# A five-layer graph transformer on one core: edge one-hots built once and loaded from DRAM in each layer

## What is computed

```python
k = typed_linear(x, ntype, Wk).reshape(n, H, HD)
q = typed_linear(x, ntype, Wq).reshape(n, H, HD)
v = typed_linear(x, ntype, Wv).reshape(n, H, HD)
kw = typed_linear_heads(k[src], etype, att)
a = jnp.sum(kw * q[dst], axis=-1) * pri[:, etype].T / np.float32(np.sqrt(HD))
amax = jax.ops.segment_max(a, dst, num_segments=n)
ae = jnp.exp(a - amax[dst])
w = ae / jax.ops.segment_sum(ae, dst, num_segments=n)[dst]
m = typed_linear_heads(v[src], etype, msg) * w[:, :, None]
h = jax.ops.segment_sum(m, dst, num_segments=n).reshape(n, D)
h = typed_linear(h, ntype, Wa)
return h * alpha + x * (1 - alpha)
```

## Time and profile before

| | us |
|---|---|
| median of 3 runs | 9909.2 |
| lowest and highest run | 9865.0, 9917.3 |
| span of the profiled execution | 9921.5 |
| PE busy | 5554.4 (56%) |
| DVE busy | 4643.5 (47%) |
| POOL busy | 4557.4 (46%) |
| ACT busy | 4066.5 (41%) |
| the five edge loops, each | 1512 to 1571 |

### The profile page before, as it was taken

One profiled execution on the slowest core, in us unless ns is written; L12 is line 12 of the kernel. 1 busy time (PEld: TensorE's weight loads), 2 busy tenths in 40 slices (PEclk: granted clock), 3 DMA queues, 4 the chain that ended last, 5 costly groups with the idle time before them and its releaser, 6 DMA issues.

```text
span 9921.5 us, 147395 instructions
## 1 busy us (share of the span) xinstructions
PE 5554.4 (56%) x33354; PEld 4735.9 (48%) x33355; DVE 4643.5 (47%) x12764; ACT 4066.5 (41%) x10084; POOL 4557.4 (46%) x4797
## 2 busy tenths in 40 slices
PE   5654545586554555955555559445454594555554
PEld 3544444464444444744444447344444573444443
DVE  5254545532555555235554552355555523555555
ACT  1244444432444444324444443344444433444442
POOL 0345555433455554335555542445555424555553
PEclk9866676797677666977666679767767796676667
DMA  2322222213222221232222213222222132222221
GB/s 69 144 62 70 70 71 70 68 70 125 69 71 72 71 72 56 100 107 72 69 72 72 69 45 124 93 69 71 70 70 71 37 140 83 73 74 73 73 76 36
DMA packets 272656, 761.00 MB, mean 77 GB/s; under 512 B 87871, under 2 KB 104356, under 8 KB 271908
## 3 DMA queue, kind: packets, MB, share of 16 engines
q0 software_dynamic: 199680, 545.53, 19.2%
q1 hardware_dynamic: 72228, 208.51, 5.4%
HBM read 557.87 MB, written 195.88 MB: 76 GB/s over the span
## 4 chain that ended last, share of the span: by engine, by line
PE 31%; another core or an unknown queue 25%; DVEq 16%; issue 12%; DVE 10%; POOLq 3%; ACT 2%; ACTq 1%; DMA 0%; POOL 0%; SPq 0%
PE ps L535 6%; PE ps L627 6%; DVEq L1061 5%; DVEq L1051 5%; PE ps L643 4%; PE ps L648 4%; PE ps L552 3%; POOLq L459 3%; DVEq L228 2%; PE ps L555 2%; PE ps L588 1%; PE ps L642 1%; DVE prod L1045 1%; DVE wmsg L1025 1%
## 5 line engine op out<-in xcount | busy, mean ns | idle before, releaser
L443 POOL DMA_INDIRECT rows<-table,idx_now x4160 | 3981.4, 957 | 3529.5 <-DVE wmsg L1029 1878.9
L642 PE MATMUL ps<-zeros,identb 128*128 128x132 bf16 x2080 | 555.0, 267 | 3189.9 <-DVE wmsg L1029 2780.9
L704 ACT ACTIVATE prod<-iota_n,dloc 128x128 bf16<-128x128 f32 x6240 | 1988.9, 389 | 106.0 <-issue 78.7
L642 PEld LDWEIGHTS ps<-zeros,identb 128*128 128x128 bf16 x2080 | 242.1, 116 | 3353.3 <-issue 3171.5
L1045 DVE TENSOR_TENSOR prod<-ps,rows 128x512 f32<-128x512 f32 x1040 | 715.5, 688 | 2352.6 <-remote 1820.4
L709 ACT ACTIVATE ohf<-prod,ones 128x512 f32<-128x512 bf16 x1040 | 750.5, 722 | 2326.4 <-remote 1887.0
L627 PE MATMUL ps<-qn,ohT 128*128 x8320 | 1583.6, 350 | 67.8 <-issue 62.7
L627 PEld LDWEIGHTS ps<-qn,ohT 128*128 128x128 f32 x8320 | 1407.3, 255 | 135.9 <-issue 129.7
L643 PE MATMUL ps<-wmsg,ohf 128*128 128x132 f32 x4160 | 1267.6, 398 | 0.0
L648 PE MATMUL ps<-wmsg,ohf 128*128 128x132 f32 x4160 | 1090.9, 355 | 0.0
L588 PE MATMUL ps<-identb,oh 128*128 128x128 bf16 x4160 | 531.8, 268 | 730.4 <-ACT ohT L721 358.8
(11 more groups left out here) (162 smaller groups left out, 6391.4 us busy)
## 6 DMA issues: line engine op xcount, KB each, us to landing
table<-rows SPq DMA_DIRECT2D x245, 768.0 KB, 3.2
rows<-table,idx_now POOLq DMA_INDIRECT x4160
out<-h SPq DMA_DIRECT2D x1, 3072.0 KB
wk<-in_L_gnn_Wk SPq DMA_DIRECT2D x20, 48.0 KB
wq<-in_L_gnn_Wq SPq DMA_DIRECT2D x20, 48.0 KB
wv<-in_L_gnn_Wv SPq DMA_DIRECT2D x20, 48.0 KB
wa<-in_L_gnn_Wa SPq DMA_DIRECT2D x20, 48.0 KB
attw<-in_L_gnn_rel_att SPq DMA_DIRECT2D x20, 24.0 KB
```

The lines of the kernel that those rows point to most:

```text
L443: pool.indirect_dma_start(out=rows[:, slot, j, :], out_offset=None, in_=table, in_offset=bass.IndirectOffsetOnAxis(ap=idx_now[:, half, c:c ...
L642: pe.matmul(bank[:, AW:2 * AW], identb[:], zeros[:], start=True, stop=True)
L704: act.activation(squares[:, turn % 2, j * P:(j + 1) * P], iota_n[:], ACT.Square, bias=dloc[:, at(4 * q + j)], scale=-1.0)
```

## The change

Everything about the one-hots leaves the edge loop. After the preparation a new stage of 208 groups, `batches`, with four buffers in the memory of `rows`, makes them once: DVE compares iota with `dloc` for four chunks in one instruction (`gen_oh`), SP stores this to `oh_d` in DRAM, PE turns it, ACT copies the turned form in bf16 (`gen_ohT`), SP stores it to `ohT_d`. In the edge loop SP loads, per position, one 128 x 512 bf16 piece of `ohT_d` for this step and one of `oh_d` for the sum two positions on, each into one of two buffers (`ohTb`, `ohb`); ACT casts each to fp32, into the same `ohT` and `ohf` as before. `dloc` moves from a buffer of its own into the memory of `rows`. SP's issues of the next layer's weights now stand ahead of the one-hot loads, and its waits for them behind the loop.

```diff
+GB = 4
+    oh_d = nc.dram_tensor("oh_d", (QUADS, P, 4 * P), BF16, kind="Internal").ap()
+    ohT_d = nc.dram_tensor("ohT_d", (QUADS, P, 4 * P), BF16, kind="Internal").ap()
...
-        oh = sb("oh", [P, 2, 4, P], BF16)
+        ohb = sb("ohb", [P, 2, 4 * P], BF16)
+        ohTb = sb("ohTb", [P, 2, 4 * P], BF16)
...
+        def batches(eng, body):
+            for k in range(GB):
+                body(k, k, 0)
+            with eng.Fori(0, QUADS // GB - 1) as it:
+                for k in range(GB):
+                    body(it * GB + (GB + k), k, it + 1)
...
             def edges_(l):
                 wa_load(l)
+                if not isinstance(l, int):
+                    weights(l + 1)
+                def body(q, slot, use, n):
+                    b = slot % 2
+                    if not beyond(q):
+                        if not is_first(q, 2):
+                            hold(sp, s_ohT, l * QUADS + q - 1)
+                        sp.dma_start(ohTb[:, b, :], ohT_d[at(q), :, :].rearrange("q p c -> (q p) c")
+                                     ).then_inc(s_ohTl[b], 16)
+                    a = summed(q + 2)
+                    if a is not None:
+                        if not is_first(a, 2):
+                            hold(sp, s_ohf, l * QUADS + a - 1)
+                        sp.dma_start(ohb[:, b, :], oh_d[at(a), :, :].rearrange("q p c -> (q p) c")
+                                     ).then_inc(s_ohl[b], 16)
+                positions(sp, body)
                 hold(sp, s_wa, l * (16 * R4) + 16 * R4)
...
+            def keep(q, b, use):
+                hold(sp, s_goh, q + 1)
+                sp.dma_start(oh_d[at(q), :, :].rearrange("q p c -> (q p) c"), gen_oh[:, b, :]).then_inc(s_gst[b], 16)
+                hold(sp, s_gohT, q + 1)
+                sp.dma_start(ohT_d[at(q), :, :].rearrange("q p c -> (q p) c"), gen_ohT[:, b, :]).then_inc(s_gst[b], 16)
+            batches(sp, keep)
+            for b in range(GB):
+                sp.wait_ge(s_gst[b], 32 * (QUADS // GB))
...
+            def turn_onehots(q, b, use):
+                pe.wait_ge(s_goh, q + 1)
+                if not is_first(q, GB):
+                    pe.wait_ge(s_gohT, q - (GB - 1))
+                for j in range(4):
+                    last = pe.transpose(ps[:, b, :].bitcast(BF16)[:, j * P:(j + 1) * P],
+                                        gen_oh[:, b, j * P:(j + 1) * P], identb[:])
+                last.then_inc(s_gtr, 1)
+            batches(pe, turn_onehots)
...
                     if not beyond(q):
-                        act.wait_ge(s_ohp, l * QUADS + q + 1)
+                        act.wait_ge(s_ohTl[b], l * (QUADS // 2 * 16) + (use * (RING // 2) + slot // 2) * 16 + 16)
                         if not is_first(q, 2):
                             act.wait_ge(s_qe, l * QUADS + q - 1)
-                        act.copy(ohT[:, b].rearrange("p s c -> p (s c)"),
-                                 ps[:, 0, :].bitcast(BF16)[:, 0:4 * P]).then_inc(s_ohT, 1)
+                        act.copy(ohT[:, b].rearrange("p s c -> p (s c)"), ohTb[:, b, :]).then_inc(s_ohT, 1)
...
                     if a is not None:
-                        onehot(ohf, a, 1 - b, turn + 1 + b, None if is_first(a, 2) else l * QUADS + a - 1).then_inc(s_ohf, 1)
+                        loads = use * (RING // 2) + (slot + 1) // 2 - LAG // 2
+                        act.wait_ge(s_ohl[1 - b], l * (QUADS // 2 * 16) + loads * 16 + 16)
+                        if not is_first(a, 2):
+                            act.wait_ge(s_agg, l * QUADS + a - 1)
+                        act.copy(ohf[:, 1 - b].rearrange("p s c -> p (s c)"), ohb[:, 1 - b, :]).then_inc(s_ohf, 1)
...
+            def make_onehots(q, b, use):
+                if not is_first(q, GB):
+                    dve.wait_ge(s_gst[b], use * 32)
+                dve.tensor_tensor(
+                    gen_oh[:, b, :].rearrange("p (s c) -> p s c", s=4),
+                    iota_n[:].rearrange("p (s c) -> p s c", s=1).broadcast_to((P, 4, P)),
+                    dloc[:, at(4 * q, 4)].rearrange("p (s c) -> p s c", c=1).broadcast_to((P, 4, P)),
+                    ALU.is_equal).then_inc(s_goh, 1)
+            batches(dve, make_onehots)
...
-                    if b == 1 and not beyond(q + 2):
-                        dve.wait_ge(s_ohp, l * QUADS + q + 1)
-                        onehot(q + 2, b).then_inc(s_oh[b], 1)
```

More of the change, by code:

```diff
@@ L182, in gnn @@
         s_gath = [sem(f"gathered{i}") for i in range(RING)]
-        s_oh = [sem(f"onehot_ready{i}") for i in range(2)]
-        s_ohp = sem("onehot_transposed")
-        s_ohT = sem("onehot_copied")
+        s_ohl = [sem(f"onehot_loaded{i}") for i in range(2)]
+        s_ohTl = [sem(f"onehot_t_loaded{i}") for i in range(2)]
+        s_ohT = sem("onehot_t_widened")
+        s_goh = sem("onehot_made")
+        s_gtr = sem("onehot_turned")
+        s_gohT = sem("onehot_t_made")
+        s_gst = [sem(f"onehot_stored{i}") for i in range(GB)]
         s_qe = sem("q_expanded")
@@ L581, in edges_ @@
             def edges_(l):
-                def turn_onehot(q, b, pair):
-                    pe.wait_ge(s_oh[b], l * (QUADS // 2) + pair + 1)
-                    if not is_first(q):
-                        pe.wait_ge(s_ohT, l * QUADS + q)
-                    pb = ps[:, 0, :].bitcast(BF16)
-                    for j in range(4):
-                        last = pe.transpose(pb[:, j * P:(j + 1) * P], oh[:, b, j, :], identb[:])
-                    last.then_inc(s_ohp, 1)
                 def softmax_piece(k, n, par):
@@ L616, in body @@
                     b = slot % 2
-                    if is_first(q):
-                        turn_onehot(0, 0, 0)
-                    if not beyond(q + 1):
-                        turn_onehot(q + 1, 1 - b, use * (RING // 2) + (slot + 1) // 2)
                     if not beyond(q):
@@ L803, in _ @@
             dve.drain()
-            dve.scalar_tensor_tensor(out=two(dloc[:]), in0=ps[:, 0:2, 0:half], scalar=float(-P),
+            dve.scalar_tensor_tensor(out=two(dloc), in0=ps[:, 0:2, 0:half], scalar=float(-P),
                                      in1=two(prep_dst()), op0=ALU.mult, op1=ALU.add)
@@ L942, in edges_ @@
             def edges_(l):
-                def onehot(q, b):
-                    for j in range(4):
-                        last = dve.tensor_scalar(oh[:, b, j, :], iota_nb[:], dloc[:, at(4 * q + j)], None,
-                                                 ALU.is_equal)
-                    return last
                 def softmax_piece(k, n, par):
```

41 lines of the change are left out of this document (14 added, 27 removed).

## The result

| | median us | lowest to highest |
|---|---|---|
| before | 9904.95 | 9865.0 to 9917.3 |
| changed | 10099.72 | 10096.5 to 10123.1 |

The ratio is 1.0201 with a 95% interval of 1.0175 to 1.0227: the change makes the kernel **2.0% slower**, where the forecast was 9800 us, 1.1% faster. The time lies in the range given and in the direction of the rivals B and C.

What follows compares the result with a forecast made beforehand. The prediction took the kernel to be bound by waiting, with TensorE's results signalled late while gathers flow. It summed 9921.5 + 260 - 395 + 20 = 9806, less 12, to say 9800 us, range 9380 to 10,250 us.

Steps and rivals of the forecast that it cites:

- Rival B: Edge loop: SP's slow load issues among the gathers make DVE or PE wait, +624 us, about 10,420 us; chance 0.16.
- Rival C: Edge loop: nothing moves, only the building shows, 10,190 us; chance 0.26 with what lies near it.
- The building: New stage before the first layer: making the one-hots once, hidden by nothing, 1.25 us per group, +260 us.
- The relief: Edge loop: less work for DVE, ACT and PE gives -0.38 us per step, -395 us in all.
- -0.24 from DVE's own time alone: Edge loop: the gain per step in us if only DVE's own saving counted, one bound of the working.
- -0.51 from the passes: Edge loop: the gain per step in us if TensorE passes are what the crawl during gathers allows.
- Rival A: Edge loop: hand-offs decide, two late signals per step instead of three, -0.89 us per step, 9265 us; chance 0.16.
- the working's lower end: Edge loop: the largest gain allowed for less work on the engines, -0.82 us per step.
- The loads: Edge loop: two one-hot loads per step, 2 x 128 KB, bandwidth not the issue, put at zero.
- A layer's start: Four of five layers: first one-hot load stands behind 21 weight issues, 50 us in; +20 us in all (0 to 60).
- The mechanism: Edge loop: while gathers flow, TensorE's results are signalled late; a step is 5.0 us of crawl and 2.4 us catching up.
- 9940 us: Whole kernel: the time if DMAs never hold TensorE back, so that only DVE's share of the gain counts.

Runs made afterwards that it cites:

- f2: The kernel before, unchanged, run again for a trace from the same chip as the other runs: 9835.9 us.
- f1: The changed kernel whole, run again on a chip with late signals: 10031.5 us, ratio 1.0189 to the kernel before.
- f3: The changed kernel with each one-hot buffer loaded once per layer, no loads in the loop, run again: 9811.1 us, ratio 0.9974 to the kernel before.
- e7: The changed kernel with the loop's one-hot loads issued by ACT behind the casts instead of by SP: 10132.1 us, ratio 1.0226 to the kernel before.
- e2: The changed kernel with only four groups of one-hots built and all loads from these at constant addresses: 9690.4 us, ratio 0.9857 to the kernel before.
- e6: The changed kernel with four groups built, loads from the same 512 KB at addresses from SP's loop register: 9792.1 us, ratio 0.9884 to the kernel before.
- e3: The kernel before with each gather replaced by an ordinary load of the same size from fixed table rows, issued by SP: 7036.9 us beside 9833.0.
- e5: The changed kernel with two gathers instead of four per step after a layer's first 16 steps: 7650.5 us beside 9833.0 for the kernel before.
- e9: The kernel before with a drain of POOL ahead of the gathers of every second step: 9084.5 us beside 9922.3; timed again, 9081.6 beside 9929.5.
- e13: The kernel before with a drain of POOL ahead of every fourth step, on the chip without late signals: 8268.5 us, ratio 1.042.

## Why the prediction was wrong, step by step

f2, f1 and f3 ran on the same chip and can be set side by side in their traces (us; product lines' starts, the five layers summed):

| | before, f2 | changed, f1 | without loads, f3 |
|---|---|---|---|
| span | 9834.1 | 10022.1 | 9807.9 |
| first product line of layer 0 | 422.4 | 706.2 | 707.1 |
| first 16 steps | 680.6 | 603.6 | 610.0 |
| middle 176 steps | 6481.0 | 6420.5 | 6218.0 |
| from there to the end of the last weighting | 658.5 | 652.7 | 649.9 |
| all between the loops and behind | 1591.6 | 1639.1 | 1622.9 |

*The building* was put at +260 us and is +273 (POOL's wait, 431.3 less 158.2). That is 1.31 us per group against 1.25, and the windows row above has no engine over 0.53 busy there (DVE, 148 of 282 us). TensorE, which turned four blocks per group, was granted 0.50 of its clock, its lower level of 1.2 GHz.

*The relief* of DVE, ACT and PE was put at -0.38 us per step, -395 in all. f3 against f2 has -263 us in the 880 middle steps, **-0.30 us per step**, and -9 behind them: -272. TensorE's lower clock is in it: in the middle of the loops the granted clock is 0.70 to 0.71 in f2 and 0.65 to 0.66 in f3. With the loads it is 0.64 to 0.66 (f1), so the loads' cost, next, is hardly the clock's. The measured relief lies between the two bounds of the working, -0.24 from DVE's own time alone and -0.51 from the passes, and nearer to the first. The term was too large by 123 us, half of that (160 x 0.38 = 61) because it was spread over all 1040 steps, though a layer's first and last ones are not of that kind. Rival A, by which the count of hand-offs decides, wanted -0.89 and falls (the working's lower end, -0.82 "below", does not agree with this -0.89). Rival C, by which nothing in the loop moves, came nearest in its time (10,190 us) and not in its mechanism: the loop moves by itself, and the loads move it back.

*The loads* were put at zero, and they are the **step that failed**: f1 less f3 is **+214 us**, 202 of it in the middle steps, 0.23 us per step. The prediction asked if SP could issue them in time and if the bandwidth sufficed. Both did: the idle time before the two casts together is 5215 us with the loads (f1) and 5240 without (f3), SP's issues of them take 0.33 us in the median (changed kernel) where 2.4 was feared in the gathers' flow, and moving them to ACT (e7) changes nothing. It did not ask what other DMAs do to the gathers' bursts and to the signals behind them. The waits in which they show are not their own. DVE's idle time in the whole span is 215 us longer in f1 than in f3 (5552 and 5337) at a busy time that differs by 5. With the loads (f1) and without (f3):

```profile
DVE prod L1020 <- remote: 454.7, 110, 5.7
...
DVE prod L1071 <- issue: 384.2, 172, 20.2
```

```profile
DVE prod L1017 <- remote: 267.7, 68, 5.6
...
DVE prod L1068 <- issue: 211.7, 58, 19.6
```

L1020 (L1017 in f3) belongs to the softmax pieces, and 143 of the 215 us stand before it: its late signals cost 187 us more with the loads, other waits there less. Another 22 stand before the pieces' first instruction. Before the product line it is 52 in all (2609 and 2557): waits that no row explains are 172 us more, those called remote (2071.7 and 2127.0) and those for PE 55 and 65 less. POOL waits 330 us longer for a free slot. What in the chip makes a load beside a gather cost this, and why loads from few addresses cost less (e2, e6), is not shown.

*A layer's start* was put at +20 us, with the first load 50 us in, and is about -28 without the loads (the first load is issued 17 us behind the first gather in layer 1): the first 16 steps are 71 us quicker, and 43 us are lost ahead of them, as the first load stands behind the weights. I had taken SP to need 2.4 us per issue there, from the earlier trace rows. In the changed kernel it does not:

```profile
2615.73 1.01 POOL L484 DMA_INDIRECT rows<-table,idx_now  x1 [0.85 <-issue]
...
2618.40 1.91 SPq L378 DMA_DIRECT2D wa<-in_L_gnn_Wa  x4
2620.50 1.90 SPq L366 DMA_DIRECT2D wk<-in_L_gnn_Wk  x4
...
2629.60 2.14 SPq L371 DMA_DIRECT2D msgw<-in_L_gnn_rel_msg  x4
...
2635.97 1.14 ACT L740 CAST ohT<-ohTb 128x512 f32<-128x512 bf16 x2 [29.28 <-issue]
```

24 issues take 13.3 us beside a gather every 1.25 us, 0.56 each. ACT and PE stand still in these 15 us, since they wait for the first load. So gathers alone do not slow SP; in the earlier trace rows gathers and working engines came together, and the prediction read the one off as the cause. In e7, where ACT loads for itself and PE works from the start, the same issues take 1.4 to 1.6 us each. Rival B stood on this price.

The four terms, 273 - 272 + 214 - 28, give 187 of the 188 us between the spans of f1 and f2; the prediction's gave -115.

*The mechanism* ahead of the sum, that TensorE's results are signalled late while gathers flow, is confirmed by e3, e5 and e9 and by the times of the raises, and bounded by e13: late signals stand in the traces of three of the four chips of the experiments. The prediction named the Trainium skill's rule that a DMA never contends with a compute engine (page "SBUF — State Buffer", section "Who interferes with whom"), which would have given 9940 us. The traces of the three chips do not contradict it for the passes, which were done in time; what comes late is their signal, of which the rule says nothing. So it does not carry the 9940 us that were drawn from it: with the gathers replaced by ordinary loads of the same bytes the kernel before takes 7037 us instead of 9833. On the fourth chip, with no remote wait before e13's product line, the trace agrees with it.

*What would show it*, as the prediction had it: the stage of about 260 us came, with gathers still every 1.25 us; ACT is far less busy; the step stayed at 7.4 us where 7.0 was wanted, and DVE's remote wait rose by a ninth where it was to fall by a fifth. B's mark, casts waiting for loads, did not show.

## What to carry to other kernels

A load that is issued and lands in time can still cost: where signals arrive late beside a DMA stream, count more DMAs as more lateness, and measure once with the loads left out before they are put at nothing. When a wait is called remote, look at when it ends and what has just stopped; here it was POOL's burst of gathers, and a drain per eight gathers was worth 8.5%, four times what the change under study moved. Then measure on more than one chip: on one without the late signals a drain per four steps only cost, 4.2%.

## What the runs showed of the hardware

- One chip ran the kernel before in 7937 us, the others in 9833 to 9930. Where it is slow, DVE waited up to 29.9 us for a signal of TensorE beside POOL's indirect gathers of 128 rows of 1 KB, one per 1.25 us; with the same bytes as ordinary DMAs (e3) it waited 2.3 us at most for TensorE before the product line.
- Late signals come in together: two that are eight passes (1.15 us) apart rose 0.09 us apart, ten to eleven microseconds after the recorded work.
- A drain of POOL behind a gather breaks its flow for 2.4 to 2.9 us, and on the chips with late signals these come in with it. Small memsets between gathers do not space them: 1.30 us instead of 1.25.
- Ordinary loads of 256 KB per step beside the gathers cost 0.23 us per step, issued by SP or by ACT, though the casts that need them idled no longer than without them (5215 and 5240 us).
- SP issued at 0.56 us each in a burst of gathers with the other engines idle, and at 2.4 us in one where they worked; in the middle of the changed kernel's loops its issues take 0.33 us in the median.
- The best version that was run is the kernel before with a drain ahead of every second step where signals are late (9082 us beside 9929), and the kernel before as it is where they are not.
